# One-sample pair products packed into three row blocks, with the last tile emptied instruction by instruction, in a recommendation tower

## The chip, the cores and the metric

The kernel runs on one core of one Trainium2 chip. The metric is the device time of one execution in microseconds (us). TensorE (PE, with its weight loads shown apart as PEld), VectorE (DVE), ScalarE (ACT) and GpSimd (POOL) compute or issue indirect DMAs; SyncE (SP) and ACT issue the other DMAs. Everything is float32; the products that pick table rows use the 32-bit replicated form (fp32r).

## The reference

For each of 512 samples, 27 embedding rows of 128 numbers are looked up in 27 tables (by `ids`), all 351 products of two different rows are formed, 16 dense features are appended, and three dense layers follow:

```python
e = jnp.stack([tbl_f[ids[:, f]] for f in range(27)], axis=1)      # 512 x 27 x 128
dot = jnp.einsum('bnd,bmd->bnm', e, e)                            # 27 x 27 products a sample
z = dot[:, j > i]                                                 # the 351 pairs
h = jnp.concatenate([z, dense_ctx], axis=1)                       # 367 features
h = jnp.maximum(h @ W_top1 + b_top1, 0.0)                         # 512 wide
h = jnp.maximum(h @ W_top2 + b_top2, 0.0)                         # 256 wide
y = h @ W_top3
```

## The kernel before

**Tiles and stages.** The 512 samples are T = 4 tiles of 128. Every feature of every sample ends in `eT`, 128 partitions (the embedding dimension) by 512 samples by 32 slots, so that one sample's 27 rows lie side by side. Features come on two ways:

- 16 features are gathered: POOL issues 64 indirect DMAs (L224), one for each tile and feature, into `E`. PE turns them in groups (`turn t g`, L272; the groups `GG` have 6, 5 and 5 features), and ACT copies each group from PSUM into `eT` (L479).
- 11 features with tables of 1000 rows are "hot". The table lies in SBUF, split by ACT (`high`, L434) and DVE (`low`, L376, with PE's `split`, L261) into two fp32r parts. DVE (`compare`, L386) and ACT (L444, L447) make one-hot columns, and PE multiplies them with both parts (`hot b c n`, L249 and L250). The 11 features are handled in six steps b: one alone, then five pairs; each step has 8 chunks c. `half_done` counts finished halves of four chunks. ACT's `copy b` (L452) moves a step's result to `eT`, and DVE's `last` (L417) moves the last feature.

**Pair products.** `dots t w` (L289): for 64 samples of tile t, PE multiplies two samples' slots (64 weight columns) with the same two samples' 27 features (54 columns). Two such products stand in the two halves of the columns of the array; what lies across the two samples isn't used. A float32 product is two passes, each a weight load and a matmul, so 32 products are 64 instructions of a kind in a call, and 512 in all. The two weight samples sit on rows 0 to 31 and 32 to 63 of a half.

**Emptying.** The first layer wants its features on partitions. Each ordered product is needed once, so of the 27 x 27 numbers ACT writes one choice of columns to `G` (`base`, L460) and DVE overwrites some of its rows by a mask (`merge`, L398). For one `dots t w` there are 4 row quadrants s and 4 target quadrants m: 16 copies on ACT and 16 masked copies on DVE. `G` has KT = 4 blocks of 128 partitions (the last uses 96), with the dense features and the bias in the last.

**Layers.** `l1 t` (L307) is 4 x 4 products of 128 x 128, thus 32 passes; `l2 t` (L320, for the last tile L320 and L329) 16 passes; `l3 t` (L338) 4 passes. `l3 0` waits until all of `G` is merged (`dots_out`), because its PSUM bank is one of the banks of `dots`. ACT applies the relus (L488, L492, L500). In the last tile `l1` and `l2` are cut in halves.

**Order.** The order on PE, DVE and ACT is written out in `PE_STEPS`, `DVE_STEPS` and `ACT_STEPS`, and every engine takes its steps strictly in that order. `HOLDS` keeps single gathers back until PE has passed a given point (`half_done`, `turn_done`, `dots_done`, and `l1_done` where so named). `pad t` (L414) zeroes the unused slots of `eT`, which are read as weights.

Of the kernel before, what the change touches and what calls it, by code (L numbers as in the profile page):

```python
# [11 lines left out]
RING = F - 1
HALF = RING // 2
COLS = HALF + 1
DENSE = 16
H1, H2 = 512, 256
N1, N2 = H1 // P, H2 // P
KT = 4
LAST_K = 96
# [6 lines left out]
GB = 8  # L26
SLOTS = 32
# [16 lines left out]
BY_ACT = [(2, 3), (3, 4), (3, 4), (3, 4), (3, 4), (3, 4)]  # L44
# [4 lines left out]
FIRST = len(PAIRS[0])  # L49

# [528 lines left out]
```

## Time and profile before

| | us |
|---|---|
| three runs of the kernel | 114.07, 115.22, 115.43 |
| median | 115.22 |
| profiled execution, its own time | 113.77 |
| its span, first to last instruction | 111.9 |
| busy in the span: PE, DVE, ACT, POOL | 99.9, 83.6, 82.9, 61.8 |

The profile describes the one execution of 113.77 us. Its span leaves out 1.9 us around the instructions. Times in the rows are microseconds from the start of the span unless marked ns. A busy PE means only that some matmul is in flight; how dense the matmuls are is seen from their number in a stretch.

### The profile page before, as it was taken

The page shows a single profiled execution, that of the slowest core. Times are in us where ns is not written, and L with a number is a line of the kernel's source. Part 1 is how long each engine was busy: PE and PEld are TensorE (multiplying, and loading weights), DVE is VectorE, ACT ScalarE, POOL GpSimd, SP SyncE. Part 2 cuts the span into 40 slices and gives each one's busy share as a digit, 9 for nine tenths or more (in the row PEclk, how much of TensorE's full clock was granted, in tenths as well). Part 3 has the DMA queues.
Part 4 walks back from the last instruction along what each step waited for, and adds up shares of the span by engine and source line. Part 5 has one row for each costly group of instructions (what it writes and reads, how often), then busy time and mean ns, then how long its engine had stood idle before and what let it go on. Part 6 is the DMA issues. An engine that isn't in the chain of part 4 may idle for free.

```text
span 111.9 us, 2572 instructions
## 1 busy us (share of the span) xinstructions
PE 99.9 (89%) x984; PEld 84.3 (75%) x984; DVE 83.6 (75%) x192; ACT 82.9 (74%) x199; POOL 61.8 (55%) x68
## 2 busy tenths in 40 slices
PE   0956999999999999999997974999999999979882
PEld 0413778878888878888775964999899999969782
DVE  5599699999999999999698079787879438960000
ACT  2568999969969999987906399499999869951230
POOL 0778677777777777777776777677770000000000
PEclk9999999999999999999999997699999999999999
DMA  2989999967944752111221132122220000000000
GB/s 40 330 316 394 342 360 341 391 212 231 270 144 107 236 179 66 48 50 47 70 51 48 47 72 54 47 53 64 57 48 23 9 0 9 0 0 0 6 0 1
DMA packets 6207, 13.33 MB, mean 119 GB/s; under 512 B 2081, under 2 KB 2849, under 8 KB 6066
## 3 DMA queue, kind: packets, MB, share of 16 engines
q1 hardware_dynamic: 3714, 8.62, 23.3%
q0 software_dynamic: 2048, 4.20, 13.6%
q10 hardware_dynamic: 432, 0.34, 1.1%
q8 instruction: 8, 0.13, 0.5%
q14 instruction: 5, 0.04, 0.1%
HBM read 13.15 MB, written 0.00 MB: 118 GB/s over the span
## 4 chain that ended last, share of the span: by engine, by line
PE 67%; DVE 13%; ACT 8%; DMA 6%; issue 2%; SPq 1%; DVEq 0%
PE ps L249 18%; PE ps L250 17%; DVE G L398 12%; PE ps L289 9%; PE ps L307 6%; DMA raw<-in_hot_rows 6%; PE ps L272 5%; ACT G L460 5%; PE ps L261 5%; PE ps L320 3%; PE ps L329 2%; PE ps L338 2%; DVE eT L417 1%; ACT hi L434 1%; SPq L183 1%
## 5 line engine op out<-in xcount | busy, mean ns | idle before, releaser
L224 POOL DMA_INDIRECT E<-in_tbl,ids_sb x64 | 61.5, 962 | 21.7 <-issue 19.2
L386 DVE TENSOR_TENSOR onehot<-idsb,ps 128x1024 fp32r<-128x1024 int16 (+1 forms) x36 | 39.2, 1123 | 2.2 <-DMA idsb<-in_ids_hot 1.2
L398 DVE COPY_PREDICATED G<-mask,ps 27x48 f32<-27x48 int32 (+1 forms) x128 | 27.1, 212 | 11.1 <-ACT G L460 9.0
L460 ACT COPY G<-ps 27x48 f32<-27x48 f32 (+1 forms) x128 | 25.2, 197 | 6.1 <-PE ps L289 4.3
L249 PE MATMUL ps<-onehot,hi 128*128 128x512 f32 x66 | 26.6, 403 | 1.2 <-DVE lo L376 1.2
L250 PE MATMUL ps<-onehot,lo 128*128 128x512 f32 x66 | 25.9, 392 | 0.0
L289 PE MATMUL ps<-eT 128*64 128x54 f32 x512 | 17.7, 234 | 3.1 <-DVE G L398 2.3
L289 PEld LDWEIGHTS ps<-eT 128*64 128x64 f32 x512 | 17.0, 148 | 4.1 <-issue 3.6
L249 PEld LDWEIGHTS ps<-onehot,hi 128*128 128x128 f32 x66 | 12.4, 188 | 5.7 <-DVE lo L376 2.8
L307 PE MATMUL ps<-G,w_sb 128*128 128x128 f32 (+1 forms) x128 | 15.2, 277 | 0.0
L444 ACT ACTIVATE onehot_a<-idsb,num 128x1024 fp32r<-128x1024 int16 (+1 forms) x12 | 13.0, 1080 | 2.6 <-PE ps L250 1.4
L307 PEld LDWEIGHTS ps<-G,w_sb 128*128 128x128 f32 (+1 forms) x128 | 14.6, 191 | 0.1
L376 DVE TENSOR_TENSOR lo<-raw,ps 128x512 fp32r<-128x512 f32 x20 | 13.6, 681 | 1.1 <-PE ps L261 0.9
L250 PEld LDWEIGHTS ps<-onehot,lo 128*128 128x128 f32 x66 | 12.4, 188 | 2.3
L434 ACT CAST hi<-raw 128x1024 fp32r<-128x1024 f32 (+1 forms) x12 | 11.5, 973 | 2.5 <-DMA raw<-in_hot_rows 1.4
L447 ACT ACTIVATE onehot_a<-onehot_a 128x1024 fp32r<-128x1024 f32 (+1 forms) x12 | 11.9, 990 | 0.4
L479 ACT COPY eT<-ps 128x640 f32<-128x640 f32 (+1 forms) x12 | 9.4, 785 | 3.2 <-PE ps L272 3.1
L452 ACT COPY eT<-ps 128x1024 f32<-128x1024 f32 (+1 forms) x6 | 8.3, 1397 | 1.9 <-PE ps L250 1.9
L272 PE MATMUL ps<-ident,E 128*128 128x128 f32 x64 | 9.1, 275 | 0.0
L249 PE MATMUL ps<-onehot_a,hi 128*128 128x512 f32 x22 | 8.8, 402 | 0.3 <-ACT onehot_a L447 0.3
L261 PE MATMUL ps<-hi,ident_r 128*128 128x512 f32 x20 | 8.3, 416 | 0.7 <-ACT hi L434 0.7
L250 PE MATMUL ps<-onehot_a,lo 128*128 128x512 f32 x22 | 8.6, 392 | 0.0
(27 smaller groups left out, 57.7 us busy)
## 6 DMA issues: line engine op xcount, KB each, us to landing
raw<-in_hot_rows SPq DMA_DIRECT2D x10, 512.0 KB, 5.9
idsb<-in_ids_hot SPq DMA_DIRECT2D x5, 256.0 KB, 7.7
E<-in_tbl,ids_sb POOLq DMA_INDIRECT x64, 2.8
w_sb<-in_w SPq DMA_DIRECT2D x1, 1024.0 KB, 7.4
w_sb<-in_w SPq DMA_DIRECT2D x1, 512.0 KB, 7.4
raw<-in_hot_rows ACTq DMA_DIRECT2D x1, 256.0 KB, 3.9
raw<-in_hot_rows SPq DMA_DIRECT2D x1, 256.0 KB, 4.1
idsb<-in_ids_hot SPq DMA_DIRECT2D x1, 128.0 KB, 3.6
```

Of the source, the lines that this page charges most:

```text
L224: pool.indirect_dma_start(out=E[:, t % ES, slot, :], out_offset=None, in_=tables[f], in_offset=bass.IndirectOffsetOnAxis(ap=ids_sb[:, t * ...
L249: pe.matmul(ps[:, HOTS[b % 2] + j, :], hi[:, k % SPLITS, rows], mine, start=(c == 0), stop=False)
L250: mm = pe.matmul(ps[:, HOTS[b % 2] + j, :], lo[:, k % SPLITS, rows], mine, start=False, stop=(c == CH - 1))
L261: pe.matmul(ps[:, ROUND, :], ident_r[:, :], hi[:, k % SPLITS, half_of(k, h)], start=True, stop=True).then_inc(split_done, 1)
L272: mm = pe.transpose(ps[:, TURN + q // 4, q % 4 * P:(q % 4 + 1) * P], E[:, t % ES, slot, :], ident[:, :])
L289: mm = pe.matmul(ps[64 * h:64 * h + 64, dots_bank(t, w) + g // GB, at:at + 2 * F], eT[:, c:c + 2, :].rearrange("p s f -> p (s f)"), eT[:, ...
L307: mm = pe.matmul(ps[:, L1_LATE if late else L1, n * P:(n + 1) * P], w1_sb[0:rows, k, n * P:(n + 1) * P], G[0:rows, k, t * P:(t + 1) * P], ...
L376: dve.tensor_tensor(lo[:, k % SPLITS, cols], raw[:, k % RAWS, cols], rounded, ALU.subtract).then_inc(lo_done, 1)
L386: dve.tensor_tensor(onehot[:, u % ONEHOTS, 0:n * B], idsb[:, k0:k0 + n, :].rearrange("p k s -> p (k s)"), ps[:, NUMBERS, c:c + 1].to_broad ...
L398: op = dve.copy_predicated(place(t, w, s, m, n), mask[32 * m:32 * m + F, m:m + 4 * (n - 1) + 1:4].unsqueeze(2).unsqueeze(3) .to_broadcast( ...
L444: act.activation(mine, idsb[:, k0:k0 + n, :].rearrange("p k s -> p (k s)"), ACT.Abs, bias=num[:, CH + c:CH + c + 1]).then_inc(away_done, 1)
L460: op = act.copy(place(t, w, s, m, n), spread(t, w, s, HALF + m, n))
```

## The change

1. **One-sample products.** `dots t w` multiplies one sample's 32 slots (32 weight columns) with its 27 features, in four column groups of the array. A call is 64 products, thus 128 passes, and all calls together 1024. Tile t has its own pair of PSUM banks (even tiles one pair, odd tiles the other), and the emptying of a tile starts after both its calls.
2. **Three row blocks.** The choice of pairs is made so that the first layer needs KT = 3 blocks: 12 blocks of 30 rows, with two features standing twice more. Slots 27 to 31 of `eT` hold copies of slots 24, 25, 26, 25 and 26 (`again 0`, `again 1`, DVE), in place of zeros. The first three hot features therefore move to slots 24 to 26. `l1` is 24 passes a tile. Dense features and bias lie in rows 30 and 31 of three quadrants and come with three DMAs in place of one.
3. **Emptying.** For one tile: 16 ACT copies of 30 x 96 numbers, 16 masked DVE copies of 30 x 96, and 4 masked DVE copies of 32 x 64. In tiles 0 to 2 DVE follows ACT by quadrant s. In the last tile they take turns by instruction: DVE's qth copy waits for ACT's qth, ACT's qth for DVE's (q - 4)th, and the four 32 x 64 copies come last.
4. **Four groups of transposes in the last tile**: 6, 5, 3 and 2 features.
5. **First loads reordered**: both halves of the first hot table are issued by ACT; SP issues the second table ahead of the second block of ids; ACT's one-hot columns of step 0 are chunks 6 and 7 in place of 2 and 3.
6. **New orders and holds** for all four engines.

The core of the diff:

```diff
@@ constants
-KT = 4
-LAST_K = 96
-GB = 8
+BLOCKS = 12
+ROWS_USED = 30
+OWN = 2 * BLOCKS
+AGAIN = [OWN, OWN + 1, OWN + 2, OWN + 1, OWN + 2]
+KT = 3
+GB = 16
-ORDER = GAT_F + HOT_F
+ORDER = GAT_F + HOT_F[3:] + HOT_F[:3]
-GG = [list(range(a, b)) for a, b in [(0, 6), (6, 11), (11, 16)]]
+GG = [[list(range(a, b)) for a, b in zip((0, *ends), ends)] for ends in [[6, 11, 16]] * (T - 1) + [[6, 11, 14, 16]]]
-BY_ACT = [(2, 3), (3, 4), (3, 4), (3, 4), (3, 4), (3, 4)]
+BY_ACT = [(6, 7), (3, 4), (3, 4), (3, 4), (3, 4), (3, 4)]
@@ PE_STEPS, the end (before and after)
-    split 10 0, hot 4 6 2, turn 1 2, hot 5 0 1, split 9 1, hot 5 1 2, split 10 1, hot 5 3 3, turn 2 0, hot 5 6 2,
-    turn 2 1, dots 0 0, dots 0 1, turn 2 2, dots 1 0, dots 1 1, l1 0, turn 3 0, dots 2 0, dots 2 1, turn 3 1, l1 1,
-    turn 3 2, l2 0, dots 3 0, dots 3 1, l1 2, l2 1, l3 0, l1 3, l2 2, l2 3, l3 1, l3 2, l3 3""")
+    hot 4 4 3, split 10 0, hot 4 7 1, turn 1 1, hot 5 0 1, turn 1 2, split 9 1, hot 5 1 2, split 10 1, hot 5 3 5,
+    turn 2 0, dots 0 0, dots 0 1, dots 1 0, turn 2 1, turn 2 2, dots 1 1, l1 0, dots 2 0, turn 3 0, dots 2 1,
+    turn 3 1, l1 1, turn 3 2, l2 0, turn 3 3, dots 3 0, dots 3 1, l2 1, l1 2, l3 0, l3 1, l2 2, l1 3, l2 3, l3 2,
+    l3 3""")
@@ DVE_STEPS, beginning and end
-    pad 0, compare 0 0 2, compare 0 4 2, low 0 0, compare 0 6 2, pad 1, low 0 1, low 1 0, compare 1 0 1, low 2 0,
+    compare 0 0 3, low 0 0, compare 0 3 2, low 0 1, compare 0 5 1, low 1 0, compare 1 0 1, low 2 0, compare 1 1 1,
-    compare 5 0 3, low 9 1, low 10 1, compare 5 5 3, pad 2, pad 3, last, dots 0 0 0 4, dots 0 1 0 4, dots 1 0 0 4,
-    dots 1 1 0 4, dots 2 0 0 4, dots 2 1 0 4, dots 3 0 0 4, dots 3 1 0 4""")
+    compare 5 6 1, low 10 1, again 0, compare 5 7 1, again 1, last, dots 0 0 4, dots 1 0 4, dots 2 0 4, dots 3 0 16""")
@@ ACT_STEPS, the end
-    turn 1 1, high 10 1, compare 5 3, compare 5 4, copy 4, turn 1 2, turn 2 0, copy 5, turn 2 1, dots 0 0 0 4,
-    dots 0 1 0 4, dots 1 0 0 4, turn 2 2, dots 1 1 0 4, l1 0, turn 3 0, dots 2 0 0 4, dots 2 1 0 2, turn 3 1,
-    dots 2 1 2 1, turn 3 2, dots 2 1 3 1, l2 0, l1 1, dots 3 0 0 4, dots 3 1 0 4, l1 2, l2 1, l1 3, l2 2, l2 3""")
+    copy 3, compare 5 3, turn 1 1, compare 5 4, turn 1 2, copy 4, copy 5, turn 2 0, dots 0 0 2, turn 2 1, dots 0 2 2,
+    turn 2 2, dots 1 0 4, turn 3 0, l1 0, dots 2 0 2, turn 3 1, dots 2 2 1, l1 1, turn 3 2, turn 3 3, l2 0,
+    dots 2 3 1, dots 3 0 9, l2 1, dots 3 9 5, l1 2, dots 3 14 2, l2 2, l1 3, l2 3""")
@@ HOLDS, gathers 49 to 63
-    47: ("half", 12), 48: ("turn", 8), 49: ("dots", 1), 51: ("dots", 2), 53: ("turn", 9), 55: ("dots", 3),
-    58: ("dots", 4), 61: ("turn", 10), 63: ("dots", 5)}
+    43: ("turn", 6), 45: ("half", 11), 48: ("half", 12), 49: ("turn", 7), 50: ("dots", 1), 51: ("dots", 2),
+    53: ("turn", 8), 54: ("turn", 9), 56: ("dots", 4), 59: ("l1", 1), 60: ("dots", 5), 61: ("turn", 10),
+    62: ("dots", 6)}
@@ sync
+                if b == 1:
+                    sp.dma_start(raw[:, k0, :], hot_rows[:, k0, :]).then_inc(raw_in[k0, 1], 16)
                 sp.dma_start(idsb[:, k0:k0 + n, :], ids_hot[:, k0:k0 + n, :]).then_inc(idsb_in[b], 16)
...
-                    sp.wait_ge(G_zero, 1)
-                    sp.dma_start(G[64:64 + DENSE + 1, KT - 1, :], dense).then_inc(dense_in, 16)
+                    sp.wait_ge(half_done, 1)
+                    for m in range(1, 4):
+                        sp.dma_start(G[32 * m + ROWS_USED:32 * m + 32, :, :], dense[m - 1]).then_inc(dense_in, 16)
@@ dots
-                v = 2 * t + w
-                if v >= 2:
-                    pe.wait_ge(dots_out, 4 * (v - 1))
-                for g in range(2 * GB):
-                    at = (g % GB) * 2 * F
-                    for h in range(2):
-                        c = t * P + 64 * h + 2 * (2 * GB * w + g)
-                        mm = pe.matmul(ps[64 * h:64 * h + 64, dots_bank(t, w) + g // GB, at:at + 2 * F],
-                                       eT[:, c:c + 2, :].rearrange("p s f -> p (s f)"), eT[:, c:c + 2, 0:F], start=True, stop=True)
+                    if t >= 2:
+                        pe.wait_ge(dots_out, 4 * (t - 1))
+                for g in range(GB):
+                    for s in range(4):
+                        c = t * P + 32 * s + GB * w + g
+                        mm = pe.matmul(ps[32 * s:32 * s + 32, DOTS[t % 2] + w, g * F:(g + 1) * F],
+                                       eT[:, c, :], eT[:, c, 0:F], start=True, stop=True)
                 mm.then_inc(dots_done, 1)
@@ merge (DVE)
+                if t == T - 1:
+                    for q in range(s0, s0 + ns):
+                        m, s = divmod(q, 4)
+                        dve.wait_ge(base_step, q + 1)
+                        dve.copy_predicated(place(t, s, m, ROWS_USED, KT), chosen(m, ROWS_USED, m, 4, KT),
+                                            spread(t, s, ROWS_USED, m, 4, KT)).then_inc(merge_step, 1)
+                    if s0 + ns == 16:
+                        for s in range(4):
+                            dve.wait_ge(merge_step, s + 1)
+                            dve.wait_ge(base_step, 13 + s)
+                            dve.copy_predicated(place(t, s, 0, 32, 2), chosen(0, 32, BLOCKS, 1, 2),
+                                                spread(t, s, 32, OWN, 1, 2)).then_inc(dots_out, 1)
+                    return
...
+                elif kind == "again":
+                    at, n = (F, 3) if x[0] == 0 else (F + 3, 2)
+                    if x[0] == 0:
+                        dve.wait_ge(hot_out, 2)
+                    dve.tensor_copy(eT[:, :, at:at + n], eT[:, :, F - n:F]).then_inc(again_set, 1)
@@ base (ACT)
+                act.wait_ge(dots_done, 2 * (t + 1))
+                if t == T - 1:
+                    for q in range(s0, s0 + ns):
+                        m, s = divmod(q, 4)
+                        if m:
+                            act.wait_ge(merge_step, q - 3)
+                        act.copy(place(t, s, m, ROWS_USED, KT),
+                                 spread(t, s, ROWS_USED, BLOCKS + m, 4, KT)).then_inc(base_step, 1)
+                    return
```

## Rows read from the trace of the kernel before

**Rows 1.** The page, part 1: busy time by engine.

```profile
PE 99.9 (89%) x984; PEld 84.3 (75%) x984; DVE 83.6 (75%) x192; ACT 82.9 (74%) x199; POOL 61.8 (55%) x68
```

**Rows 2.** Two stages: length; PE, PEld, DVE, ACT, POOL; clock, DMA.

```profile
11.26:61.75 50.49, 49.71 (x232) 39.27 (x232) 48.08 (x52) 43.01 (x43) 38.03 (x41) 1.00 0.56 176
61.75:100.20 38.45, 35.25 (x665) 34.07 (x665) 27.08 (x128) 31.25 (x140) 16.78 (x18) 0.96 0.14 35
```

**Rows 3.** Groups by line and shape: count | busy, mean ns | idle.

```profile
L289 PE MATMUL ps<-eT 128*64 128x54 f32 x512 | 17.7, 234 | 3.1 <-DVE G L398 2.3 <-DVE eT L417 0.8
...
L398 DVE COPY_PREDICATED G<-mask,ps 27x48 f32<-27x48 int32 x96 | 20.0, 208 | 1.3
...
L398 DVE COPY_PREDICATED G<-mask,ps 27x64 f32<-27x64 int32 x32 | 7.1, 223 | 9.8 <-ACT G L460 9.0
...
L460 ACT COPY G<-ps 27x64 f32<-27x64 f32 x64 | 13.1, 204 | 5.3 <-PE ps L289 4.3
...
L460 ACT COPY G<-ps 27x48 f32<-27x48 f32 x64 | 12.1, 189 | 0.7
...
L452 ACT COPY eT<-ps 128x1024 f32<-128x1024 f32 x4 | 6.1, 1525 | 0.9 <-PE ps L250 0.9
...
L414 DVE MEMSET eT<- 128x640 f32 x4 | 2.4, 592 | 0.3
```

**Rows 4.** Timeline of the start: start, length, instruction, count, idle before.

```profile
8.87 1.04 ACT L434 CAST hi<-raw 128x1024 fp32r<-128x1024 f32 x1 [1.43 <-DMA raw<-in_hot_rows]
...
12.11 1.22 DVE L386 TENSOR_TENSOR onehot<-idsb,ps 128x1024 fp32r<-128x1024 int16 x1 [0.92 <-PE ps L250]
...
14.98 0.68 DVE L376 TENSOR_TENSOR lo<-raw,ps 128x512 fp32r<-128x512 f32 x1
```

**Rows 5.** Timeline where the hot stage ends.

```profile
55.36 3.47 DVE L386 TENSOR_TENSOR onehot<-idsb,ps 128x1024 fp32r<-128x1024 int16 x3
...
60.36 1.17 DVE L417 COPY eT<-ps 128x512 f32<-128x512 f32 x1 [0.17 <-PE ps L250]
...
61.78 3.94 PE L289 MATMUL ps<-eT 128*64 128x54 f32 x128 [0.81 <-DVE eT L417]
```

**Rows 6.** L289 alone in stretches that grow from 89.40; columns as before.

```profile
89.40:89.62 0.22, 0.17 (x6) 0.17 (x7) 1.00 0.00 0
89.40:89.66 0.26, 0.21 (x6) 0.21 (x8) 1.00 0.00 0
...
89.40:89.68 0.28, 0.23 (x8) 0.23 (x9) 1.00 0.00 0
```

**Rows 7.** Stretches around an idle PE; all engines.

```profile
66.43:68.60 2.17, 0.00 (x1) 0.03 (x1) 1.99 (x10) 2.03 (x11) 1.78 (x2) 1.00 0.24 64
...
68.72:72.13 3.41, 3.41 (x64) 3.30 (x63) 3.16 (x15) 1.80 (x10) 2.50 (x3) 0.50 0.20 52
```

**Rows 8.** The last gathers (issue part, timeline), and two layer steps.

```profile
E<-in_tbl,ids_sb POOLq DMA_INDIRECT x64, 2.8
...
82.76 0.94 POOL L224 DMA_INDIRECT E<-in_tbl,ids_sb  x1 [0.30 <-issue]
...
86.91 0.58 PEld L272 LDWEIGHTS ps<-ident,E 128*128 128x128 f32 x5
...
96.89 1.87 PEld L320 LDWEIGHTS ps<-raw,w_sb 128*128 128x128 f32 x16
...
100.22 3.65 PEld L307 LDWEIGHTS ps<-G,w_sb 128*128 128x128 f32 x32
```

**Rows 9.** Timeline of the last emptying and of what follows.

```profile
91.57 6.75 ACT L460 COPY G<-ps 27x64 f32<-27x64 f32 x32 [0.90 <-PE ps L289]
...
92.42 7.31 DVE L398 COPY_PREDICATED G<-mask,ps 27x64 f32<-27x64 int32 x32 [2.02 <-ACT G L460]
...
99.78 0.52 PEld L338 LDWEIGHTS ps<-wb_sb,raw 128*128 128x128 f32 x4 [1.03 <-DVE G L398]
...
109.90 0.16 ACT L506 COPY y<-ps 128x4 f32<-128x4 f32 x1 [0.87 <-PE ps L338]
```

More of the change, by code:

```diff
@@ L49 @@
 FIRST = len(PAIRS[0])
+assert HOT % 2
 F32 = mybir.dt.float32
@@ L506, in _, with pair @@
             act.copy(y[:, :], ps[:, L3, 0:T]).then_inc(y_out, 1)
-def column_mask():
-    mask = np.zeros((4, 32, HALF), np.int32)
-    for k in range(HALF):
-        mask[:, k + 1:k + HALF + 1, k] = 1
-    return mask.reshape(P, HALF)
-def first_layer_rows():
-    rows = np.full((32, COLS), -1)
-    for k in range(HALF):
-        for i in range(RING):
-            if i != k:
-                j = k if k + 1 <= i <= k + HALF else k + HALF
-                a, b = sorted((ORDER[i], ORDER[j]))
-                rows[i, k] = b * (b - 1) // 2 + a
-    for i in range(RING):
-        a, b = sorted((ORDER[i], ORDER[RING]))
-        rows[i, HALF] = b * (b - 1) // 2 + a
+def first_layer_rows():
+    take = np.zeros((BLOCKS + 2, 32), np.int32)
+    rows = np.full((BLOCKS, 32), -1)
+    def pair(i, j):
+        a, b = sorted((ORDER[i], ORDER[j]))
+        return b * (b - 1) // 2 + a
+    for k in range(BLOCKS):
+        for i in range(ROWS_USED):
+            if i < OWN:
+                other, second = i % BLOCKS, i >= BLOCKS
+                take[k, i] = second if other <= k else not second
+                if i == k + BLOCKS:
+                    continue
+            else:
+                take[k, i] = i < F
+            slot = i if i < F else AGAIN[i - F]
+            if i == k:
+                take[k, i] = 0
+            rows[k, i] = pair(slot, k if take[k, i] else BLOCKS + k)
+    for n, i in ((0, 30), (0, 31), (1, 31)):
+        take[BLOCKS + n, i] = 1
+        rows[4 * n, i] = pair(AGAIN[i - F], OWN + n)
     assert sorted(rows[rows >= 0]) == list(range(F * (F - 1) // 2))
-    return rows
+    return take, rows
 def kernel(**inputs):
@@ L536 @@
     W1 = np.asarray(inputs["W_top1"])
-    rows = first_layer_rows()
+    take, rows = first_layer_rows()
     w1 = np.zeros((4, 32, KT, H1), W1.dtype)
-    for k in range(COLS):
-        used = rows[:, k] >= 0
-        w1[k % 4, used.nonzero()[0], k // 4] = W1[rows[used, k]]
-    w1[2, 0:DENSE, KT - 1] = W1[F * (F - 1) // 2:]
-    w1[2, DENSE, KT - 1] = np.asarray(inputs["b_top1"])
-    ids = np.asarray(inputs["ids"]).reshape(2, 2, P // 4, T, F).transpose(0, 2, 1, 3, 4)
+    for k in range(BLOCKS):
+        used = rows[k] >= 0
+        w1[k % 4, used.nonzero()[0], k // 4] = W1[rows[k, used]]
+    rest = np.zeros((3 * 2 * KT, H1), W1.dtype)
+    rest[0:DENSE] = W1[F * (F - 1) // 2:]
+    rest[DENSE] = np.asarray(inputs["b_top1"])
+    w1[1:, ROWS_USED:] = rest.reshape(3, 2, KT, H1)
+    mask = np.zeros((4, 32, BLOCKS + 2), np.int32)
+    for m in range(4):
+        mask[m] = take.T
+    ids = np.asarray(inputs["ids"])
     numbers = CH * np.arange(P)[:, None] + np.arange(CH)
@@ L564 @@
         "eye": np.eye(P, dtype=np.float32),
-        "mask": column_mask(),
+        "mask": mask.reshape(P, BLOCKS + 2),
     }
```

130 lines of the change are left out of this document (62 added, 68 removed).

## The prediction

> **What bounds the kernel now.** I read the page's busy times first, then busy time by stage, the groups by shape, and the timeline of both ends of each stage. PE is busy for 89% [rows 1], yet the other engines stand at 74 and 75%, so the stages have to be told apart. In the hot stage, 11.3 to 61.8 us, PE is busy for 49.7 of 50.5 us and DVE for 48.1 [rows 2]: both bind it. In the tail, 61.8 to 100.2 us, PE has 35.3 of 38.5, ACT 31.3, DVE 27.1. There DVE and ACT follow PE's `dots`: for each `dots t w` ACT needs 16 copies and DVE 16. The last two calls together took ACT 6.75 and DVE 7.31 us [rows 9], thus 0.211 and 0.228 us a copy, 3.4 and 3.65 us a call. PE needs 1.9 us for it (128 passes, two calls, in 3.94 less some 0.2 of the last one's flight) [rows 5]. The end is a chain: `dots 3` from 89.45 to 93.3, emptying to 99.73 (92.42 + 7.31), then `l3 0`, `l1 3`, `l2`, `l3` and `y` at 110.06 [rows 9]. The gathers stand close behind: the last is issued at 82.76 and, with the median 2.8 us to landing, is there at 85.6; its transposes ran at 86.91 [rows 8].
>
> **Price 1, a pass of one-sample `dots`, decides.** The trace has no 32-column product. A pass with 128 weight columns takes 3.65/32 = 114 ns [rows 8]. With 64 columns and two column groups, 29.2 ns: passes 6 and 8 end a pattern in which two start within some 10 ns and then none for 40 (six at 89.62, still six at 89.66, eight at 89.68) [rows 6], and 128 passes are spread over 3.74 us. So a column group takes a pass every 58 ns at 64 columns and every 114 ns at 128: in proportion to the weight columns. Both passes of a product stand in one group, in order, so two groups overlap, not four. At 32 columns that makes about 26 ns from the first pass to the second, and the 6 ns or so to the next group stay: 32 ns for two, 16.3 ns a pass, 2.09 us a call of 128 passes. Ends: 14.6 ns (all of it halves, 1.87 us) and 29.2 ns (nothing halves, 3.74 us). I take 16.3, as both widths shown lie on one line through nearly zero.
>
> The Trainium skill speaks against this: "TensorE: Matmul & The Clock Gate", section "Wait — 56ns, not 53.3ns?", says that start to start never falls below about 25 ns however small the matmul. By that, a call would be an estimated 3.2 us. The starts some 10 ns apart in [rows 6] disagree with it for two column groups, but no row shows a mean below 29.2.
>
> **Price 2, the emptying.** ACT: 48 numbers 189 ns, 64 numbers 204 [rows 3], 0.94 ns each, so 96 numbers 234 ns, with the 7 to 11 ns between copies 0.245. DVE: 208 and 223, so 253 for 96, at its pitch 0.27; the 32 x 64 copy 0.26 with its wait. A tile then costs ACT 16 x 0.245 = 3.9 us (before 6.75) and DVE 16 x 0.27 + 4 x 0.26 = 5.4 (before 7.3). Over four tiles ACT loses 11 us and DVE 8, nearly all beside PE. Ends: 10% either way, -0.5 to +0.9 us at the end of the kernel.
>
> **Price 3, layer 1**: 24 passes for 32, 2.74 for 3.65 us, 0.9 a tile, of which the last tile's lies bare.
>
> **Price 4, the hot stage.** PE has the same passes. At the start the 0.92 us that DVE idled before 12.11, the 1.43 that ACT waited for the second table [rows 4], and one `pad` (0.59) [rows 3] go, or mostly so; SP now waits for the first `half_done` (near 10 us) ahead of the dense rows, with the weights, the mask and the ids and tables of step 3 on behind it, and issues two DMAs more; the table after those is used after 20 us and the weights at 62, so up to 3 us late cost nothing, and beyond that PE would wait as long as they are late. I give DVE 1.0 us, `low 1 1` ending at 14.7 for 15.66 [rows 4] (ends 0 and 1.5). At the end `again 0` stands ahead of the last compare. Its 512 groups of three: a copy with groups of two took ACT 1.525 us [rows 3]; bounds are the plain rate of the `pad` (592 ns for 640, so 1.4 us for 1536) and three single-slot copies of 1.17 [rows 5], 3.5. I take 1.75. Before, compares ended at 58.83 (55.36 + 3.47) and `last` started 1.5 later, since PE had half a step and six transposes to do; now PE waits with only the last chunk left, 4 passes of 0.23 and 0.2 of flight. So 58.83 - 1.0 + 1.75 + 1.2 = 60.8, and `dots 0 0` 1.42 later, as before (60.36 to 61.78) [rows 5]: 62.2. If DVE's smaller waits vanish too, 61.2. I take 61.7, no gain. `again 1` runs while PE does that last chunk.
>
> **The tail, step by step**, with those prices, turns at 0.11 to 0.12 us a transpose (0.58 for 5) [rows 8] and ACT's copy of them 0.8. `dots 0` both calls end at 65.9. ACT empties half, waits for `turn 2 1`, empties the rest; `turn 2 2` waits 1 us for ACT. `dots 1` ends at 72.2, tile 0 is merged at 73.2, so `l1 0` waits 1 us and ends at 76.0. `dots 2` ends at 80.8, `l1 1` at 84.1, and PE reaches `turn 3 3` at 86.3. That is the gathers' point as well (85.6): an earlier PE gains 0.7 at most here. The holds don't bite: gather 60 needs `dots 2 0`, 78.3, and its time is 79.0 (three gaps of 1.25 ahead of 82.76); gather 62 needs 80.8 and has 81.5. After two transposes and ACT's copy `dots 3` starts at 87.3 and ends at 91.5 (before 93.3).
>
> Last tile: ACT starts at 91.7; DVE follows 0.3 later and is the slower of the two, so neither new wait (ACT's for the copy four back, DVE's for ACT's) bites until q = 8; `l2 1`'s relu sits between q 8 and 9 and `l1 2`'s, which waits for PE, between 13 and 14, so q 14 and 15 come at 97.0 and 97.2; four more copies: `dots_out` full at 98.7 (before 99.73). PE has finished `l2 1` and `l1 2` at 96.1 and idles 2.6 us, because `l3 0` waits for the last merge. Then `l3 0`, `l3 1` 0.9, `l2 2` 1.9, `l1 3` 2.7, `l2 3` 1.9, `l3 2` and `l3 3` with ACT's relu before the last 1.3: `y` at 107.5, against 110.06. The sum is -2.6 us: 111.2 for the profiled 113.77. The three runs have their median at 115.22, 1.45 above it; the same saving gives 115.2 - 2.6 = 112.6.
>
> **Rivals.**
>
> *A, the sum holds*: 112.6 us, chance 0.38. For it: the proportion in price 1.
>
> *B, the clock falls before the last layers.* After PE had idled 2.17 us (66.43 to 68.60) its clock went from 2.4 to 1.2 GHz and stayed for 3.4 us, in which 64 passes were in flight where 117 fit [rows 7]; the 0.8 us idle ahead of 61.78 brought no fall. My walk has a PE idle for 2.6 us at 96.1, and all behind it is PE's. Half of 3.4 us lost: +1.6, 114.2 us. In return the fall at 68.7 goes, which the walk has already left out. Chance 0.24.
>
> *C, a pass costs PE its issue, not its columns.* For it: twice as many passes, each with its own weight load, and no row below 29.2 on the mean. At 29.2 all eight calls grow by 1.65 us less the gathers' 0.7: +12, 125 us; at 20.3 ns (2.6 a call) `y` comes at 111.0, +1.0. The point from which it decides: 2.46 a call, 19 ns, there the change gains nothing. Chance 0.22, of which 0.17 slower by over 2%. The skill's 25 ns, named above, is this rival's likeliest form: by my walk an estimated 5.3 us later than before, 120.5, chance 0.12 within these.
>
> *D, the expected gain is hidden anyway*: `again 0` at its upper price (+1.7) or a late start eats it; 113.5 to 115, chance 0.06.
>
> *E, more is gained than I count*: four groups overlap, or DVE keeps all of its 1.5 us at the start and PE reaches the last gather early; then gathers set `dots 3` at 86.6 and short passes and emptying save 1 more: 110.5 to 111.5. Chance 0.10.
>
> **How the numbers follow.** About 2% (2.3 us, 112.9) is what a measurement of this kernel can tell from no change. A lies just beyond it; of its 0.38 I put 0.29 faster and 0.09 within, so faster is 0.29 + 0.10 and some of B's 0.03: 0.42. Within 2%: 0.09 + 0.21 + 0.05 + 0.06 = 0.41. Slower 0.17. The range runs from 110.5 (E) to 117.5 (C up to 22 ns), leaving out most of C's slow part and 0.04 below. A's own range is 111.8 to 113.6.
>
> **What would show it.** L289's new group: its 1024 passes in calls of 2.1 us prove price 1; 3.2 or 3.7 prove C. L460's and L398's successors at 234 and 253 ns prove price 2. `dots 0 0` near 61.7 proves price 4; ACT's `turn 3 3` near 87 with PE waiting for a gather says that the gathers bind. PEclk at half after 98 us says B. I am wrong if the calls are much over 2.1 us, or if PE is not idle ahead of `l3 0`.

## The result, and the profile after

| | us |
|---|---|
| changed kernel, four runs | 122.31, 122.50, 122.87, 123.25 |
| median, changed and before (four runs each) | 122.69 and 114.85 |
| ratio to before, with its 95% interval | 1.073 [1.068, 1.079] |
| predicted | 112.6, range 110.5 to 117.5 |
| profiled execution; its span; mean granted clock | 122.87; 121.0; 0.915 (before 0.985) |

The change costs 7.8 us where 2.6 were to be gained. The page after: busy time, the clock by slices (here the whole line), the queue of instruction DMAs, and the largest new groups.

```profile
PE 98.7 (82%) x1464; PEld 82.0 (68%) x1464; DVE 75.6 (62%) x142; ACT 71.2 (59%) x136; POOL 62.7 (52%) x68
...
PEclk9999999999999999999999955579999965798599
...
q8 instruction: 11, 0.18, 0.7%
...
L297 PE MATMUL ps<-eT 128*32 128x27 f32 x1024 | 13.7, 200 | 11.1 <-issue 9.5
```

DVE and ACT have less to do than before [rows 1], as the change means them to. PE's busy time is nearly as before too. What is new is in L297, the one-sample `dots` (L289 before): 13.7 us busy, less than before's 17.7 [rows 3], but 11.1 us idle ahead of its passes, and of these 9.5 are "issue", time in which PE waited for nothing that the profile shows. The clock is at half in three places where before had one. PE's timeline, from the first `dots` to the end of the kernel, shows where (start, length, line, tiles, shapes, count, idle before and what ended it):

```profile
61.33 3.30 PE L297 MATMUL ps<-eT 128*32 128x27 f32 x221 [0.74 <-DVE eT L442]
65.61 1.81 PE L297 MATMUL ps<-eT 128*32 128x27 f32 x128 [0.98 <-issue]
69.61 0.50 PE L297 MATMUL ps<-eT 128*32 128x27 f32 x35 [2.19 <-issue]
70.04 1.22 PE L281 MATMUL ps<-ident,E 128*128 128x128 f32 x5
72.15 1.30 PE L281 MATMUL ps<-ident,E 128*128 128x128 f32 x5 [0.89 <-ACT eT L512]
73.38 1.52 PE L297 MATMUL ps<-eT 128*32 128x27 f32 x82
75.97 0.85 PE L297 MATMUL ps<-eT 128*32 128x27 f32 x46 [1.07 <-issue]
76.75 4.69 PE L314 MATMUL ps<-G,w_sb 128*128 128x128 f32 x24
...
92.65 1.27 PE L297 MATMUL ps<-eT 128*32 128x27 f32 x126 [0.46 <-ACT eT L512]
95.65 1.31 PE L297 MATMUL ps<-eT 128*32 128x27 f32 x128 [1.73 <-issue]
99.38 0.31 PE L297 MATMUL ps<-eT 128*32 128x27 f32 x2 [2.42 <-issue]
99.62 3.79 PE L327 MATMUL ps<-raw,w_sb 128*128 128x128 f32 x16
103.20 3.39 PE L314 MATMUL ps<-G,w_sb 128*128 128x128 f32 x24
109.14 1.05 PE L345 MATMUL ps<-wb_sb,raw 128*128 128x1 f32 x8 [2.55 <-DVE G L412]
```

Two things are to be seen. First, the passes come in bursts, and the counts repeat. Between the stalls at 65.61 and 69.61 lie 128 passes; between 69.61 and 75.97 lie 35 + 5 + 5 + 82 = 127; in the last tile again 128. A pass is two instructions of PE, a weight load and a matmul, so PE stops every 256 instructions. Counted over all of PE's instructions in the trace (weight loads, matmuls, and 64 others, nearly all of them semaphore waits), the stalls stand behind 961, 1217, 1473, 1985, 2497 and 2753 instructions, all 256 or 512 apart. The queue "instruction" moved 0.18 MB in 11 packets, 16 KB each, against 8 before; 2 x 1464 and 2 x 984 instructions [rows 1] in parts of 256 make 11.4 and 7.7. Second, in a burst a pass is far cheaper than any price in the prediction, but over a block it is not. The whole of the last tile's `dots` (length, then busy time with count of PE, PEld, DVE, ACT, POOL; clock; DMA share and GB/s):

```profile
92.65:99.69 7.04, 2.90 (x257) 2.63 (x257) 1.30 (x5) 1.40 (x6) 0.00 (x0) 0.84 0.02 5
```

126 passes in 1.27 us give 10 ns each at most. Yet the 256 passes of `dots 3` took 7.04 us, 27.5 ns each, and from one resume to the next (95.65 to 99.38) 128 passes took 3.73 us, 29 ns each. That is nearly the 3.74 us over which the prediction spread 128 passes of before (3.94 [rows 5] less the last one's flight).

The packets of the instruction queue can be placed in time. After 92 us the only traffic in this stretch is theirs, so the column with the DMA share shows them. Columns as above:

```profile
92.65:92.78 0.13, 0.13 (x15) 0.13 (x18) 0.00 (x0) 0.13 (x2) 0.00 (x0) 1.00 0.00 0
92.78:94.18 1.40, 1.14 (x126) 1.03 (x122) 0.03 (x1) 1.27 (x6) 0.00 (x0) 1.00 0.06 12
94.18:95.65 1.47, 0.00 (x0) 0.00 (x1) 1.26 (x5) 0.00 (x0) 0.00 (x0) 1.00 0.00 0
95.65:96.68 1.03, 1.03 (x118) 1.03 (x120) 0.00 (x0) 0.00 (x0) 0.00 (x0) 1.00 0.00 0
96.68:97.98 1.30, 0.28 (x34) 0.18 (x20) 0.00 (x0) 0.00 (x0) 0.00 (x0) 0.82 0.06 13
97.98:99.38 1.40, 0.00 (x1) 0.00 (x1) 0.00 (x0) 0.00 (x0) 0.00 (x0) 0.50 0.00 0
```

One packet of 16 KB moves from 92.79 to 94.17 us, and PE goes on at 95.65; the next moves from 96.69 to 97.97, and PE goes on at 99.38. All six stalls of this trace end so, 1.2 to 1.5 us after a packet of that queue has arrived.

The last emptying and the end, from ACT's and DVE's timelines:

```profile
99.73 2.27 ACT L488 COPY G<-ps 30x96 f32<-30x96 f32 x9 [5.61 <-PE ps L297]
...
104.09 1.24 ACT L488 COPY G<-ps 30x96 f32<-30x96 f32 x5
...
119.05 0.16 ACT L539 COPY y<-ps 128x4 f32<-128x4 f32 x1 [0.47 <-PE ps L345]
```

```profile
108.10 0.98 DVE L412 COPY_PREDICATED G<-mask,ps 32x64 f32<-32x64 int32 x4
```

### The profile page after: what moved, and what is told of

Same layout as the page of the kernel before. It is cut to its first block, busy times and chain, and to the rows that moved or that the text cites. A ratio compares the mean times of both kernels' runs of the same rounds, so it can differ in the third digit from the quotient of the medians.

```text
span 121.0 us, 3427 instructions
## 1 busy us (share of the span) xinstructions
PE 98.7 (82%) x1464; PEld 82.0 (68%) x1464; DVE 75.6 (62%) x142; ACT 71.2 (59%) x136; POOL 62.7 (52%) x68
## 4 chain that ended last, share of the span: by engine, by line
PE 67%; issue 11%; DVE 11%; DMA 5%; ACT 3%; ACTq 1%; DVEq 0%
PE ps L258 13%; PE ps L259 13%; PE ps L314 12%; PE ps L297 11%; PE ps L327 7%; DVE onehot L393 5%; PE ps L281 5%; DMA ident<-in_eye 5%; PE ps L270 4%; DVE lo L383 4%; PE ps L345 2%; PE ps L336 1%; ACT hi L460 1%; DVE eT L442 1%; ACT eT L512 1%
## 5 line engine op out<-in xcount | busy, mean ns | idle before, releaser
L418 DVE COPY_PREDICATED G<-mask,ps 30x96 f32<-30x96 int32 x48 | 12.5, 261 | 19.1 <-ACT G L493 11.8
L297 PE MATMUL ps<-eT 128*32 128x27 f32 x1024 | 13.7, 200 | 11.1 <-issue 9.5
L297 PEld LDWEIGHTS ps<-eT 128*32 128x32 f32 x1024 | 11.7, 115 | 13.6 <-issue 12.7
L493 ACT COPY G<-ps 30x96 f32<-30x96 f32 x48 | 11.0, 230 | 8.6 <-PE ps L297 8.0
L512 ACT COPY eT<-ps 128x640 f32<-128x640 f32 (+3 forms) x13 | 9.6, 741 | 9.0 <-PE ps L281 8.9
L314 PE MATMUL ps<-G,w_sb 128*128 128x128 f32 x96 | 14.7, 323 | 0.0
L314 PEld LDWEIGHTS ps<-G,w_sb 128*128 128x128 f32 x96 | 14.5, 241 | 0.1
L281 PE MATMUL ps<-ident,E 128*128 128x128 f32 x64 | 10.4, 298 | 0.9 <-ACT eT L512 0.9
L281 PEld LDWEIGHTS ps<-ident,E 128*128 128x128 f32 x64 | 8.0, 151 | 2.7 <-issue 2.0
L406 DVE COPY_PREDICATED G<-mask,ps 30x96 f32<-30x96 int32 x16 | 4.2, 260 | 8.4 <-ACT G L488 8.0
L478 ACT COPY eT<-ps 128x1024 f32<-128x1024 f32 (+1 forms) x6 | 6.6, 1103 | 4.4 <-PE ps L259 4.4
```

Source lines behind the costliest of these rows:

```text
L281: mm = pe.transpose(ps[:, TURN + q // 4, q % 4 * P:(q % 4 + 1) * P], E[:, t % ES, slot, :], ident[:, :])
L297: mm = pe.matmul(ps[32 * s:32 * s + 32, DOTS[t % 2] + w, g * F:(g + 1) * F], eT[:, c, :], eT[:, c, 0:F], start=True, stop=True)
L314: mm = pe.matmul(ps[:, L1_LATE if late else L1, n * P:(n + 1) * P], w1_sb[:, k, n * P:(n + 1) * P], G[:, k, t * P:(t + 1) * P], start=(fir ...
L418: op = dve.copy_predicated(place(t, s, m, ROWS_USED, KT), chosen(m, ROWS_USED, m, 4, KT), spread(t, s, ROWS_USED, m, 4, KT))
```

## The experiments

The theory: **PE's instructions reach it in blocks of 256, and a run of short products uses them up faster than they come**, at one block in about 3.7 us. The idle gaps that result bring the clock down, and the longer path behind carries it to the end. The rivals: a short pass costs PE more by itself (C of the prediction), by its columns or by its four column groups, or the new orders do the harm.

### Three shapes of product, and the kernel before with the new product

e1 has half as many instructions, each with twice the moving columns; e2 keeps the number of the instructions and doubles their moving columns; e3 has half as many with 64 weight columns. These three show times only: each leaves half of the needed products out or forms them from the wrong samples. e4 forms all of them and puts the new product alone into the kernel before. The core of each edit:

```diff
@@ e1_half_instructions
-                for g in range(GB):
+                for g in range(0, GB, 2):
...
-                                       eT[:, c, :], eT[:, c, 0:F], start=True, stop=True)
+                                       eT[:, c, :], eT[:, c:c + 2, 0:F], start=True, stop=True)
@@ e2_moving54 (all 1024 passes, 54 moving columns for 27)
+                        r = c // 2 * 2
...
+                                       eT[:, c, :], eT[:, r:r + 2, 0:F], start=True, stop=True)
@@ e3_wide64 (512 passes, 64 weight columns for 32)
-                    for s in range(4):
-                        c = t * P + 32 * s + GB * w + g
+                    for h in range(2):
+                        c = t * P + 64 * h + 2 * (GB * w + g)
...
+                                       eT[:, c:c + 2, :].rearrange("p s f -> p (s f)"), eT[:, c, 0:F],
...
@@ e4_before_one_sample (on the kernel before)
-                    for h in range(2):
+                    for s in range(4):
...
+                                       eT[:, c, :], eT[:, c, 0:F], start=True, stop=True)
```

> The changed kernel with every other product of dots left out: each remaining one multiplies one sample's 32 slots with two samples' 54 columns, so 512 passes in place of 1024, 32 weight columns and the PSUM space as in the changed kernel; half of the products are missing and what stands in their places is wrong. Theory S (PE runs out of instructions: they arrive in blocks, and 256 passes of dots take some 7 us however short each is): the idle stretches inside dots vanish, y comes near 106.8 us of the span, 111 us in all. Theory G (the array is slow with four column groups of 32, or falls to the low clock in that mode): the gaps stay in part, 117 to 120 us.

> The changed kernel with all 1024 passes, but each multiplies with 54 columns (two samples) in place of 27, so twice the column work with the same number of instructions; part of the products are wrong. Theory S: no change, within 1% of the changed kernel's 122.7 us, since the time of a call is set by the arrival of instructions and not by the columns. Theory G: each pass gets longer, some 11 ns by 1024, and it is 128 to 134 us.

> The changed kernel with passes of the old width of weights: 64 weight columns (two samples) and 27 moving columns, 512 passes, in two column groups; half of the products are of the wrong pair of samples. It gives the changed kernel a dots call of the old price, 1.87 us. By the sum of my prediction with that price and the measured copies y comes at 107.6, 111.5 us in all (S). If the rest of the change is what costs (turn-taking, new orders, holds), it stays at 118 or more.

> The kernel before with one part of the change alone: dots in one-sample products, 1024 passes of 32 weight columns and 27 moving columns, in the old PSUM places, order and packing. Theory S: a tile's dots takes about 7 us in place of 3.9, four times, some of it hidden behind emptying: 119 to 125 us. If the loss comes from the new order and the emptying instead, it is 114 to 116.

| | passes of `dots` | us, median | ratio to before (114.37) |
|---|---|---|---|
| e1, 32 x 54, half of them | 512 | 110.31 | 0.969 [0.960, 0.978] |
| e2, 32 x 54 | 1024 | 118.69 | 1.040 [1.030, 1.050] |
| e3, 64 x 27 | 512 | 112.02 | 0.979 [0.974, 0.984] |
| e4, before with 32 x 27 | 1024 | 120.21 | 1.058 [1.051, 1.064] |

e1 and e3 have half the instructions with different columns, and the loss is gone in both (e1 has one stall left in `dots`, of 0.92 us); e2 doubles the moving columns of the changed kernel and is 4.0 us *faster*, where theory S had no change and G a loss, so columns do not set the time of `dots`. e4 has none of the new orders, packing or emptying and is 5.8 us slower than before, so most of the loss comes with the product alone. In e4 the stalls stand behind 961, 1217, 1473, 1985 and 2753 instructions (and a short one of 0.26 us behind 2497), the same counts as in the changed kernel, though the steps there are others. e2's last tile stalls at the same two places as the changed kernel's, and takes no more time for twice the moving columns (7.02 us, 91.90 to 98.92, for 7.04):

```profile
91.90 1.72 PE L298 MATMUL ps<-eT 128*32 128x54 f32 x126 [0.46 <-ACT eT L513]
94.90 1.73 PE L298 MATMUL ps<-eT 128*32 128x54 f32 x128 [1.28 <-issue]
98.63 0.28 PE L298 MATMUL ps<-eT 128*32 128x54 f32 x2 [2.00 <-issue]
98.85 2.05 PE L328 MATMUL ps<-raw,w_sb 128*128 128x128 f32 x16
```

From one resume to the next it is again 3.73 us (94.90 to 98.63): the longer bursts are paid out of the stalls (1.28 for 1.73, 2.00 for 2.42 us). So the gain does not come from the passes. Between the two traces it is 3.0 us (spans of 118.0 and 121.0), 0.8 of it ahead of the end of `dots 3` and 2.2 behind it: with PE less idle, `l2 1` ran in 2.05 us at the full clock where the changed kernel had 3.79 at half.

e3 has `dots` calls of 64 passes at 64 columns, 2.05 us each with the last pass's flight, and 3.92 for two in a row, close to the price that the prediction put on them (2.09 and 4.2). It is therefore the test of everything else in the sum:

```profile
72.19 2.92 PE L315 MATMUL ps<-G,w_sb 128*128 128x128 f32 x24 [1.04 <-DVE G L424]
...
86.74 3.92 PE L297 MATMUL ps<-eT 128*64 128x27 f32 x128 [0.46 <-ACT eT L513]
90.59 2.05 PE L328 MATMUL ps<-raw,w_sb 128*128 128x128 f32 x16
92.48 2.84 PE L315 MATMUL ps<-G,w_sb 128*128 128x128 f32 x24
97.88 1.10 PE L346 MATMUL ps<-wb_sb,raw 128*128 128x1 f32 x8 [2.55 <-DVE G L413]
98.84 3.61 PE L328 MATMUL ps<-raw,w_sb 128*128 128x128 f32 x16
```

No stall is left within `dots`. And 27 moving columns are no faster than before's 54: 128 passes in 3.92 us, where [rows 5] had 3.94.

### Moving the block boundaries

If the boundaries lie at fixed counts of PE's instructions, what stands in front of `dots` decides where they fall. e5 takes four instructions out of the warm-up; e6 adds 92 (23 products of 32 x 1, four instructions each).

```diff
@@ e5_one_warmup_less
-WARM = 2
+WARM = 1
@@ e6_shift_92, behind the warm-up
+            for _ in range(23):
+                pe.matmul(ps[0:32, TURN, 0:1], G[:, 0, 0:32], G[:, 0, 0:1], start=True, stop=True)
```

> The changed kernel with one warm-up product (4 PE instructions, some 57 us ahead of the first dots) left out. The stalls of the changed kernel sit exactly 256 PE instructions apart (counts 961, 1217, 1473, 1985, 2497, 2753 at the restart), and the last tile's dots has 126 + 128 + 2 passes: it needs a third block for its last two. Theory S (instructions come in blocks of 256): with all of PE's program four places earlier the 256 passes end with the second block, the last stretch of 2 passes with 2.4 us ahead goes, and the time falls by 1.8 to 2.7 us, to 120 to 121. Theory G (four column groups, clock, or waits in dots): the place in the program means nothing, 122.7 us, within 0.4.

> The changed kernel with 23 tiny products (92 PE instructions, 32 x 1 columns) behind the warm-up ones, while PE has nothing else to do. Theory S: all block borders move 92 places towards the front of the work; the last tile's dots then starts with 80 passes left of a block and the next block already there, and its passes end some 1.8 us earlier, 120 to 121.5 us; the stalls restart at the same counts plus 0, that is at the same counts of PE instructions from the start. Theory G: 122.7 us or a little more.

e5: 122.21 us, 1.067 [1.061, 1.073] of before's 114.45, where 120 to 121 were expected: a miss in the total. In the last tile the boundaries moved as foretold, by two passes, so that `dots 3` was whole after 4.0 us instead of 7.0. But the stall did not go: it stands, 2.57 us long, ahead of `l2 1`, still behind 2753 instructions:

```profile
94.50 1.29 PE L297 MATMUL ps<-eT 128*32 128x27 f32 x128 [0.46 <-ACT eT L512]
97.23 1.29 PE L297 MATMUL ps<-eT 128*32 128x27 f32 x128 [1.44 <-issue]
101.08 3.75 PE L327 MATMUL ps<-raw,w_sb 128*128 128x128 f32 x16 [2.57 <-issue]
```

What ACT and DVE gained by the earlier `dots 3` came to nothing, since everything here had begun 1.85 us later (94.50 for 92.65; the first `dots` 0.8 us later, at 62.10, and a longer half-clock stretch, 69.4 to 83.1 for 70.2 to 80.4).

e6: 118.74 us, 1.029 [1.020, 1.039], so 92 useless instructions made the kernel about 4 us faster, more than the 1.2 to 2.7 expected: the stall behind 1473 instructions went as well, and `l1 0` took 2.92 us at the full clock for 4.69. The stalls stand behind the same counts (961, 1217, 2241, 2753), and in the last tile the boundary falls after 80 and 208 passes, as expected; by the first of them the next block was there:

```profile
90.44 1.98 PE L297 MATMUL ps<-eT 128*32 128x27 f32 x208 [0.46 <-ACT eT L514]
94.93 0.62 PE L297 MATMUL ps<-eT 128*32 128x27 f32 x48 [2.51 <-issue]
```

208 passes in 1.98 us are 9.5 ns a pass, with no stall: the price of a pass where instructions are at hand. Crossing into a block asks for the next one: the boundary after 80 passes was crossed near 91.2, the queue's packet moved from 92.51 to 93.39, and PE went on at 94.93, 3.7 us behind the crossing. This also says why some boundaries show no stall, as that at 1729 in the changed kernel: the block before it held `l1 0` and lasted from 75.97 to 82.2, longer than a fetch. Neither columns nor the order of the steps explains either run. The spacing of 256, the stalls that keep their count when other work is put in front, and the packet that arrives ahead of each resume are what the block theory needs.

The Trainium skill has a matching note ("Advanced Engine Details and Errata", section "ISA Cache"): the instruction cache of TensorE has 128 KB, a line of it is 16 KB, thus 256 instructions, and "Only 2 cache lines!" The runs agree with the 256 and the 16 KB; how many lines are held no run here tests. The time that a line takes to come, 3.4 to 4.3 us from one resume to the next where `dots` fills the block between, is measured here and not stated there.

### The end of the kernel

The prediction had PE idle for 2.6 us ahead of `l3 0`, and rival B a clock that falls there. e7 takes e3 and puts `l3 0` behind `l2 2` and `l1 3`, so that PE has work during the last merges; e8 does the same to the changed kernel.

```diff
@@ e7, e8: the end of PE_STEPS
-    l2 1, l1 2, l3 0, l3 1, l2 2, l1 3, l2 3, l3 2, l3 3
+    l2 1, l1 2, l2 2, l1 3, l3 0, l3 1, l2 3, l3 2, l3 3
```

> The kernel of e3 (512 passes of 64 weight columns, half of the products wrong) with one change in PE's order at the end: l2 1, l1 2, l2 2, l1 3, l3 0, l3 1, l2 3, l3 2, l3 3, so that l2 2 fills the idle time in which l3 0 waited for the last merge. In e3 PE idled 2.55 us there, its clock fell to half for 3.4 us right after, and l2 2 took 3.4 us for 1.87. If the idle time and the fall are what cost (my rival B), l2 2 moves ahead (about 1 us gained after its own wait for a relu), l3 0 and 1 lie under the relu of l1 3, and the clock stays up: 2 to 3.5 us less than e3, 108.5 to 110. If the clock falls whatever stands there: 110.5 to 111.5.

> The changed kernel with the other order of PE's last steps alone (that of e7). The price of rival B on the changed kernel itself: in e7 it was 3.5 us (112.0 to 108.5). Expected 119.2 to 120.5 us; if the instruction stalls keep the clock down anyhow, 121 to 122.

e7: 108.53 us, 0.945 [0.939, 0.951] of before, 3.5 us under e3 (like e3 it forms half of the products wrongly, so this is no time of a usable kernel), with the clock at full speed in the whole span. Its end:

```profile
91.09 2.05 PE L328 MATMUL ps<-raw,w_sb 128*128 128x128 f32 x16
92.98 2.84 PE L315 MATMUL ps<-G,w_sb 128*128 128x128 f32 x24
96.60 2.02 PE L328 MATMUL ps<-raw,w_sb 128*128 128x128 f32 x16 [0.78 <-ACT raw L522]
98.46 2.88 PE L315 MATMUL ps<-G,w_sb 128*128 128x128 f32 x24
101.17 0.95 PE L346 MATMUL ps<-wb_sb,raw 128*128 128x1 f32 x8
```

The idle 2.55 us of e3 is down to 0.78, `l2 2` takes 2.02 us for 3.61, and `l3 0` comes when the merges have long been done. e8 can't be set against the changed kernel in microseconds, since it ran in another set (below); its ratio to before is 1.036 against 1.073. It was expected at 119.2 to 120.5 us beside a before of 114.5; how much of that difference the place of the steps makes isn't told apart from the set.

### Putting them together

e9 is e8 with e6's 92 instructions. e10 is e9 with the last tile in two-sample products. e11 has tiles 1 and 3 so, with a few steps and holds moved to fit. e12 is e9 again. All of them form all products.

```diff
@@ e10, e11: dots of a two-sample tile, over all four banks
+                    for g in range(GB):
+                        for h in range(2):
+                            c = t * P + 64 * h + 2 * (GB * (1 - w) + g)
+                            at = g % 8 * 2 * F
+                            mm = pe.matmul(ps[64 * h:64 * h + 64, DOTS[1 - w] + g // 8, at:at + 2 * F],
+                                           eT[:, c:c + 2, :].rearrange("p s f -> p (s f)"), eT[:, c:c + 2, 0:F],
+                                           start=True, stop=True)
```

> The two corrections together: the 92 tiny instructions ahead (e6, 4.0 us) and the other end (e7, 3.5 us). If they add up, 115.2 us, else 115.5 to 117. Still slower than the kernel before (114.5), since 1024 passes still arrive in blocks of 256 instructions.

> As e9, and the last tile's dots in two-sample products (64 weight columns, 54 moving), 128 passes over four PSUM banks, the first half in the banks that are free, the second after tile 2 is merged; its copies have the same number of elements, written with a step of two columns. The last tile then needs 256 PE instructions for 512 and no block arrives inside it with nothing before. Sum: dots 3 from 90.4 to 94.3, and from its end to the end of y 13.9 us as in e7: 110.1 in all of the span, 112 us, 2% less than the kernel before. If strided writes or the wait for tile 2 cost more, 113 to 115.

> The changed kernel with the other end order and 92 more small products after the warm-up, and tiles 1 and 3 back in products of two samples (64 weight columns by 54, a group of products in each half of the array, four banks), tiles 0 and 2 in one-sample products; ids of tiles 1 and 3 are placed so that the evictions write without a step. 1536 TensorE instructions of the dots instead of 2048. Theory of the arrival of instructions (blocks of 256 at about 3.7 us): two blocks fewer, so one or two of the stalls of 1.0 to 2.5 us go, and the clock stays up longer: 2 to 3.5 us under e12 beside it, at or a little under the kernel before (ratio 0.98 to 1.00). Theory of columns: tiles 1 and 3 carry more column work again, so no gain over e12 or a loss of up to 2 us. The stretch that decides is the last tile's: 128 passes in 3.7 to 3.9 us against 4.2 us with its stall.

> The kernel of e9 again (the changed kernel, other end order, 92 small products of 32 x 1 after the warm-up), because the kernel before was itself 15 per cent slower than usual beside e9. If the gains of e6 (4.0 us) and e7 (3.5 us) add: 115.2 us beside a kernel before of 114.5 to 115, ratio 1.00 to 1.01. If they overlap (both take away the same cold stretch before the last layers): 117 to 118.7 us, ratio 1.02 to 1.03. If place does not matter and e6 was chance: 119 us, ratio 1.04.

In the two sets of runs from which these come, the kernel before itself took 131.7 us, so only ratios to it and differences within a set are used. In the traces of these sets the hot stage is longer: the first `dots` begins at 73.3 us in e12 and at 75.2 in e8, instead of 61.3. What holds it up isn't settled, and there is no trace of the kernel before from these sets. So a ratio here compares two hot stages as well, and need not hold where before takes 114.5 us.

| | set | us, median | ratio to before |
|---|---|---|---|
| e8, other end | 1 | 136.93 | 1.036 [1.024, 1.049] |
| e9, other end and 92 more | 1 | 132.66 | 1.012 [1.005, 1.020] |
| e10, last tile two-sample | 1 | 133.07 | 1.015 [1.008, 1.021] |
| e11, tiles 1 and 3 two-sample | 2 | 138.05 | 1.050 [1.043, 1.058] |
| e12, e9 again | 2 | 131.65 | 1.006 [1.002, 1.011] |

- e9 against e8: 4.3 us by the 92 instructions alone, as e6 showed (4.0 us).
- e12 is e9's kernel, and the best version that leaves nothing out: the two sets put it at 1.012 and 1.006 of before, so in these sets it wins back nearly all of the 7.3% and gains nothing. Its expectation had 1.00 to 1.01 if the gains of e6 and e7 add.
- e10 met its expectation that the stall within `dots 3` goes, and still gained nothing. Its `dots 3` took 5.0 us (109.79 to 114.79) for e9's 4.9 (109.09 to 113.94), since it needs both pairs of banks and waited 0.84 us for the merges of tile 2. And DVE's 16 masked copies of the last tile wrote their target with a step of two numbers and took 368 ns each instead of 260; of these 16 x 0.11 = 1.7 us, 0.8 are seen at the end (14.7 us from the end of `dots 3` to `y` for 13.9).
- e11 was expected to gain 2 to 3.5 us on e12 and lost 6.4. Its two-sample tiles take all four PSUM banks, so the next `dots` waits for a whole emptying, and the previous one for the same. PE's idle time ahead of them:

```profile
88.96 3.32 PE L306 MATMUL ps<-eT 128*64 128x54 f32 x55 [2.92 <-issue]
...
100.35 1.68 PE L314 MATMUL ps<-eT 128*32 128x27 f32 x132 [3.06 <-DVE G L442]
```

Both starts lie 0.05 and 0.15 us behind the last merge copy of a tile on DVE (88.68 + 0.23 and 99.97 + 0.23), although the first is put down to "issue". These 6 us are a cost of the buffers in my version and say nothing of the block theory. The stretch that was to decide, the last tile's `dots`, took 4.5 us (115.79 to 120.27), expected at 3.7 to 3.9, for e12's 4.7 (109.09 to 113.75). A mix with banks enough for both forms was not tried.

## Why the prediction was wrong

The walk through the tail, against the changed kernel and e3 (us from the start of the span):

| | predicted | changed | e3 |
|---|---|---|---|
| first `dots` begins | 61.7 | 61.3 | 61.1 |
| `dots 1` ends | 72.2 | 76.8 | 71.2 |
| `l1 0` ends | 76.0 | 81.4 | 75.1 |
| `l1 1` ends | 84.1 | 89.9 | 83.3 |
| `dots 3` begins | 87.3 | 92.7 | 86.7 |
| `dots 3` ends | 91.5 | 99.7 | 90.7 |
| last merge ends | 98.7 | 109.1 | 97.8 |
| `y` ends | 107.5 | 119.2 | 108.0 |

**Price 1 is the step that failed**, both in its reasoning and in its claim that it had bounds. It priced a pass by its weight columns, took 16.3 ns, and put 14.6 and 29.2 ns as the ends. In a burst the truth lies below the lower end (9.5 ns: passes in different column groups overlap more than the text's "two groups overlap, not four" allowed), and over a run of calls near the upper one (27.5 ns in `dots 3`). The prediction asked what a pass costs the array and put the arrival of the instructions at nothing; the runs showed that it sets the time, at one block of 256 in about 3.7 us. The hint stood in the trace of before: 128 passes in 3.74 us are 256 instructions in 3.74 us, just the rate at which blocks come, so before ran at the edge of it, and the packets of the instruction queue were on the page. By the end of `dots 3` the walk is 8.2 us late (99.7 for 91.5), 1.8 of them by way of the clock, since `l1 0` took 4.69 us for 2.92; rival C would have set 8 x 1.65. (The working of price 1 also gives 32 / 2 = 16.0 ns and not 16.3, which changes nothing.)

**The clock**, which the sum had left out, follows from it up to the last merge. In the changed kernel it stood at half (1.2 GHz) from 70.2 to 80.4, 97.5 to 104.3 and 111.2 to 114.6 us, behind or during long stalls of PE (67.42 to 69.61; 93.92 to 95.65 and 96.96 to 99.38; 106.59 to 109.14). `l1 0` took 4.69 us for 2.92 in e3, `l2 1` 3.79 for 2.05. Since `l2 1` and `l1 2` hold up ACT's relus, and these the copies behind them, the last emptying grew from the predicted 7.2 us to 9.4 (99.7 to 109.1). From there to the end of `y` it was 10.1 for 8.8. So 8.2 + 2.2 + 1.3 = 11.7 us, the difference of `y`. The last 1.3 us do not come from price 1: e3, which has no stalls in `dots`, needs the same 10.1 us there. They are rival B's.

**Rival B** was right in its mechanism: with price 1 mended (e3), PE idles 2.55 us ahead of `l3 0`, as the text said, and `l2 2` behind it took 3.61 us at half clock for 1.95. e7 removed the idle time and gained 3.5 us, twice what B was given (1.6); part of that is the order itself, as PE works during the 2.55 us, and the two parts weren't told apart.

**Rival C** had the right outcome in sign, with 0.17 for slower by over 2%, and the wrong mechanism: e2 shows that a pass as such is cheap. The Trainium skill's floor of 25 ns from start to start ("TensorE: Matmul & The Clock Gate", section "Wait — 56ns, not 53.3ns?"), which the prediction called C's likeliest form, is contradicted here for products in different column groups: 9.5 ns a pass over 208 passes. That the time came near to what the prediction had by this floor (an estimated 120.5) is a coincidence; moving the boundaries changes the time by 4 us at the same number of passes, which no floor would.

**What held.** Price 2: ACT's copies took 230 ns (234 said), DVE's 260 (253), the 32 x 64 ones 222. Price 3: `l1` 2.84 to 2.92 us at the full clock (2.74). Price 4: `dots 0 0` at 61.3 (61.7); there `again 0` was dearer in the text (1.75 us) than on the chip (1.20). PE's idle time ahead of `l3 0`, 2.55 us (2.6). With 64-column products nearly the whole walk holds, up to the last merge (97.8 for 98.7). That e3 took 112.02 us for the predicted 112.6 is in part luck: it is 0.9 us early there, with `dots` calls a little cheaper than 2.09, and loses 1.3 us behind it to the clock that the sum left out. The gathers, which the text had arriving just as PE needs them for `dots 3`, did not set it in the changed kernel: the last was issued at 88.00 instead of 82.76 [rows 8], because its hold waited for the late `dots`.

**What stays open.** What exactly sets a fetch off: behind a stall the next packet mostly starts 1.0 to 1.8 us after PE has gone on, but behind that at 69.61 us, where PE soon waited for ACT, 3.5 us after (73.07). Open is also how the fetch shares the DMA engines with gathers, since in the slower sets PE also paused for 0.4 us after every four to six passes in parts of `dots` (in e12 at 89.43, 90.16 and 90.89 us), which no block boundary explains, and how much of the loss left in e12 is the stall of 2.06 us that its `dots 3` still has.

## What to carry to other kernels

Count instructions as well as work: where a change trades one product for several small ones, compare instructions per microsecond with the best sustained rate that the trace shows (here 256 in about 3.7 us, 14.6 ns each, weight loads counted), over any run of more than about 256 of them. A group with low busy time and much "issue" ahead of it, with pauses at equal counts of instructions, is short of instructions, not of data; half as many, wider products take the stalls away (e3, e7; e1 keeps one of 0.9 us), and small shifts of the program can move the time by some per cent. No version here forms the products of all tiles in the wide form and keeps the new packing: a whole wide product moves 54 columns, in before at the same 3.94 us for 128 passes as e3's 27, but needs twice the room in PSUM, which cost e11 its gain. And keep PE supplied with independent work during a last emptying: taking away 1.8 of 2.55 idle microseconds gained 3.5 us in e7, since the clock stayed up.

## What was not expected of the hardware

- Passes of 32 weight columns in four column groups ran at 9.5 ns each (208 in 1.98 us); at 54 moving columns at 13.5 ns (128 in 1.73 us); at 64 weight columns in two groups at 30.6 ns (128 in 3.92 us), with 27 moving columns as with 54 (3.94 in before). All with the last pass's flight.
- 92 more instructions at the start: 118.74 us for 122.69, by ratio to before 1.029 for 1.073.
- A gather's time on POOL, 0.94 us as a rule, was 1.94 us beside DVE's copy within SBUF (`again 0`, 1.20 us) and 1.45 beside `again 1`:

```profile
55.91 1.94 POOL L233 DMA_INDIRECT E<-in_tbl,ids_sb  x1 [0.31 <-issue]
58.15 1.45 POOL L233 DMA_INDIRECT E<-in_tbl,ids_sb  x1 [0.30 <-issue]
```

- A masked copy of 30 x 96 on DVE took 260 ns with adjacent targets and 368 ns with a step of two (e10); e11, which reads PSUM in the same pattern and writes without a step, has 260.
